# First mixer of a four-stage block: the squares of the queries move from ScalarE to GpSimd, and the first state of the chain of chunks is written with four copies in place of sixteen

## The chip, the core and the metric

The kernel runs on one core of a Trainium2 chip. A core has TensorE (PE; its weight loads are listed as PEld), VectorE (DVE), ScalarE (ACT), GpSimd (POOL) and SyncE (SP), each with an instruction queue of its own, and they meet through semaphores: an instruction can wait for a semaphore to reach a value (`wait_ge`) and can raise one when it ends (`then_inc`). The metric is the time of one execution in microseconds (us). The median of three executions of the kernel before is 836.53 us.

## What is computed

The reference runs four sublayers on 2 sequences of 512 tokens with 256 features, each with a layer norm ahead and a residual sum behind: a mixer with a delta rule, a mixture of experts, a causal attention, and a second mixture of experts. The change lies in the first. There, 16 heads of 16 features:

```python
q = _short_conv(hidden @ Wq, conv_wq)      # conv over 4 tokens, then silu; k and v alike
beta = sigmoid(hidden @ Wb)
q = _l2norm(q) * Dk ** (-0.5)              # x * rsqrt(sum(x*x) + 1e-6) over a head's 16 features
k = _l2norm(k)
def step(S, inp):
    qt, kt, vt, bt = inp
    u = vt - einsum('bhk,bhkv->bhv', kt, S)
    S = S + bt * kt[..., None] * u[..., None, :]
    return S, einsum('bhk,bhkv->bhv', qt, S)
o = _rmsnorm(o, norm_w) * sigmoid(hidden @ Wg)
x = x + o @ Wo
```

The sum of the squares of q that the norm needs is what the moved instructions prepare.

## The kernel before

All instruction streams are written out by hand, one Python function for each engine, and the order in a function is the order in that engine's queue. The first mixer is in `make_attn0`. It cuts the 512 tokens into 32 chunks of 16 and has these stages.

Up to 50 us: projections by TensorE, the short convolution by VectorE, SiLU by ScalarE (`silu_q`, line 2399, writes the queries `qn_`), grams of the chunks. ScalarE, VectorE and TensorE are all full. GpSimd builds masked keys (line 2590) and squares the keys (line 2598), `sq[0]`, with the same operation that the change uses for the queries. Queries and keys stand interleaved in one tile `qk`, so that each is read with a step of two elements.

55 to 92 us, where the change is:
- VectorE runs the elimination, a loop `for m in range(CH + 2)`, which inverts the chunks' triangular systems. Each turn has up to four `tensor_tensor` operations (lines 2780, 2788, 2794 and 2798), all of two inputs from SBUF, with 120 to 512 elements a partition; each waits for a result of the ones ahead of it. The sizes rise to the middle of the loop and fall again.
- TensorE makes the key places, eight groups `u` (line 2227) into banks 6 and 7 in turn, and ScalarE copies each out (line 2454). Among these copies ScalarE has the two squares of the queries, `sq[1]` (line 2457), behind u = 2 and u = 5. Then it takes a square root (line 2459), copies the queries to `qc` (line 2474), which SyncE spreads by 16 DMAs (line 2098), and takes the results of the elimination out of PSUM (`ft_out`, line 2469) and the gates (line 2463).
- TensorE, behind the key places: the first of eight groups of transposes `turn_ft` (line 2251), the sums over the squares (line 2131, 32 matmuls of 8 columns, which wait for `s_sqq`), two further `turn_ft`, and then gates (line 2241) and `turn_ft` in turn. `turn_ft(i)` waits for the turn of the elimination that makes its data; the last waits for VectorE's last step.
- GpSimd clears a tile (line 2612), clears `hdiag` and `seed`, writes `seed`, the first state of the chain (line 2620, 16 copies of 32 partitions x 16 elements, four for each `h`, with a memset of `hdiag` ahead of each four), multiplies for `wz` (line 2626, waits for ScalarE's square root), waits for the gates, and clears `ub` and `place` (lines 2630 and 2631).

From 92 us: `spread(i)` on VectorE, ScalarE and GpSimd (lines 2820, 2501, 2645) waits for the last `ft_out`, for VectorE's small copy at line 2805 and for the sums of the squares, `units(i)` on TensorE (line 2287) waits for the spreads, and then the 32 chunks follow one another in a chain over TensorE, ScalarE and VectorE (lines 2314, 2330, 2863, 2868), to about 190 us. The other three sublayers (`make_rest`) follow.

`ft_out` writes a tile `ftc` that lies over `qk`. So the queries must have been read when the first `ft_out` runs. Before the change all of their readers stand ahead of it in ScalarE's own queue.

Of the kernel before, what the change touches and what calls it, by code (L numbers as in the profile page):

```python
# [11 lines left out]
KD = DIM // P  # L12
# [4 lines left out]
H0, D0, CONV = 16, 16, 4  # L17
# [35 lines left out]
ALU = mybir.AluOpType  # L53
ACT = mybir.ActivationFunctionType
# [1837 lines left out]
def make_attn0(nc, io, sem, sb, arena, bank, rest, g):  # L1892
# [9 lines left out]
    xnT, xn, ident, headmask, w0, wo0, conv_w, norm_w = (  # L1902
        g[n] for n in ("xnT", "xn", "ident", "headmask", "w0", "wo0", "conv_w", "norm_w"))
# [3 lines left out]
    def at(off, n):  # L1907
        assert off + n <= ARENA
        return arena[:, off:off + n]
# [9 lines left out]
    qn_, kc = qk[:, :, :, 0], qk[:, :, :, 1]  # L1919
# [3 lines left out]
    sq = [at(XO + 8192 + NP * t, 2048).rearrange("p (a t) -> p a t", a=KD) for t in range(2)]  # L1923
# [15 lines left out]
    seed = w0f[:, 1024:1280]  # L1939
# [25 lines left out]
    s_siq = sem("a0_siq")  # L1965
    s_siv = sem("a0_siv")
    s_sqk = sem("a0_sqk")
    s_sqq = sem("a0_sqq")
# [118 lines left out]
    class Attn0:  # L2087
# [283 lines left out]
        def act(self, act):  # L2371
# [64 lines left out]
            for i in range(8):  # L2436
# [4 lines left out]
                if g2:  # L2441
# [3 lines left out]
                    for j in range(j0, j0 + 4):  # L2445
                        ins = nc.scalar.copy(ful[1][:, j:CH, :, j].rearrange("p r c -> p c r"), pul[:, j, :, j:CH])
# [5 lines left out]
            for u in range(8):  # L2452
                act.wait_ge(s_kqm, u + 1)
                nc.scalar.copy(kq[:, u, :], bank[6 + u % 2][:]).then_inc(s_kqe, 1)
                if u in (2, 5):
                    act.wait_ge(s_siq, 2)
                    nc.scalar.activation(sq[1][:, u // 3, :], qn_[:, u // 3, :], ACT.Square).then_inc(s_sqq, 1)
            act.wait_ge(s_w, 3)
            nc.scalar.activation(kn[:], rkn[:], ACT.Sqrt).then_inc(s_srk, 1)

# [5 lines left out]
            def ft_out(i):  # L2466
                y, r0, n = i % 2, i // 2 * 4, 2 if i == 7 else 4
                act.wait_ge(s_ft, i + 1)
                nc.scalar.copy(ftc[:, :, y, r0:r0 + n].rearrange("p u r -> p r u"),
                               b_ft[i % 3][:, 0:n * P].rearrange("p (r u) -> p r u", r=n)).then_inc(s_fta, 1)  # L2470

            for a in range(KD):
                for u in range(2):
                    ins = nc.scalar.copy(qc[:, a, :].rearrange("p (n v u x) -> p n v u x", n=NT, v=2, u=2)[:, :, :, u, :],
                                         qn_[:, a, :].rearrange("p (n u v x) -> p n u v x", n=NT, v=2, u=2)[:, :, u, :, :])
            ins.then_inc(s_qc, 1)
            act.wait_ge(s_qc, 1)
            for i in range(3):
                ft_out(i)
            gates(0)  # L2480
# [40 lines left out]
            for c in range(NCH):  # L2521
                t, c8, par, u, s = c // 8, c % 8, c % 2, c // 4, c // 2 % 2
                if c < NCH - 1:
                    for h in range(2):
# [5 lines left out]
                        rows = slice(s * 32, s * 32 + 32)  # L2530
                        src = uo[h][s][rows, 0:256].rearrange("p (j b n) -> p j b n", j=2, b=2)[:, :, 0, :]
                        dst = ub[s][rows, 2 * h:2 * h + 2, 0:64]
                        if par:
                            ins = nc.scalar.activation(dst, src, ACT.Copy, scale=evod[rows, 1:2])
                        else:
                            ins = nc.scalar.copy(dst, src)
# [3 lines left out]
                if par:  # L2540
                    for h in range(2):
# [3 lines left out]
                        for b in range(BATCH):  # L2545
                            o = b * 64 + (1 - s) * 32
                            pr = c8 // 2
                            ins = nc.scalar.copy(
                                fin[t % 2].rearrange("p (b q n) -> p b q n", b=2, q=4)[pr * 32:pr * 32 + 32, b, 2 * h:2 * h + 2, :],
                                uo[h][s][o:o + 32, 0:256].rearrange("p (j b n) -> p j b n", j=2, b=2)[:, :, b, :])  # L2550
# [16 lines left out]
        def act_std(self, act, t):  # L2567
            act.wait_ge(s_fss, 2 * t + 2)
            nc.scalar.activation(fst[1], fst[0], ACT.Sqrt).then_inc(s_fsd, 1)

        def act_turn(self, act, t):
            act.wait_ge(s_ftt, t + 1)
            nc.scalar.copy(fyt, b_fin[:]).then_inc(s_fte, 1)

        def pool(self, pool):
# [8 lines left out]
            for e in range(8):  # L2584
                a, t = e // 4, e % 4
# [3 lines left out]
                for h in KBP:  # L2589
                    ins = nc.gpsimd.tensor_scalar(  # L2590
                        kbd[e % 3][:, :, :, h, :],
                        kc[:, a, :].rearrange("p (b t c j) -> p b t c j", b=BATCH, t=4, c=8)[:, :, t, :, :],
                        hmc(h), 1.0, ALU.mult, ALU.mult)
                ins.then_inc(s_kbp, 1)
                if e in (3, 5):
                    a = (e - 3) // 2
# [7 lines left out]
            for r in range(CH):  # L2604
                ins = pool.memset(ful[0][:, r, :, r:r + 1], 1.0)
# [10 lines left out]
            for h in range(4):  # L2616
                rows = slice(32 * h, 32 * h + 32)
                nc.gpsimd.memset(hdiag[rows, h, :], 1.0)
                for x in range(4):
                    ins = nc.gpsimd.tensor_copy(seed[rows, x * 64 + h * D0:x * 64 + (h + 1) * D0],  # L2620
                                                ident[rows, 32 * h + D0:32 * h + 32])
            ins.then_inc(s_seed, 1)
            pool.wait_ge(s_seed, 1)
            pool.wait_ge(s_rk, 4)
            pool.wait_ge(s_srk, 1)
            nc.gpsimd.tensor_tensor(wz[:], kn[:], beta[:], ALU.mult).then_inc(s_srk, 1)
# [364 lines left out]
```

## Time and profile before

| | |
|---|---|
| median of 3 executions | 836.53 us (835.92 to 839.29) |
| the profiled execution: its time | 836.49 us |
| its span in the trace | 834.7 us |
| busy: TensorE, VectorE, ScalarE, GpSimd | 787.2, 482.1, 360.4, 218.4 us |
| TensorE's granted clock, mean | 0.991 of full |

### The profile page before, as it was taken

Reading aid. Unit: us, or ns where it says so; the run is one execution under the profiler, and the core shown is the slowest. Engines: PE = TensorE matmul, PEld = TensorE weight load, DVE = VectorE, ACT = ScalarE, POOL = GpSimd, SP = SyncE. Lnnn points to the kernel's source line nnn. Section 1 sums busy time; section 2 is a strip of 40 time slices with the busy share of each in tenths; the row PEclk is TensorE's granted clock in tenths of the full one; section 3 lists DMA queues with packets and bytes.
Section 4 is the critical chain, followed back from the end, with each engine's and each line's share of the span. In section 5 each row is a group of like instructions: output and inputs, shape, how many; then the busy total and the mean of one; then the engine's idle time right before and its main releaser. Section 6 shows DMA issues by size and latency. Waiting matters only on the chain.

```text
span 834.7 us, 14393 instructions
## 1 busy us (share of the span) xinstructions
PE 787.2 (94%) x4825; PEld 545.6 (65%) x4825; DVE 482.1 (58%) x1167; ACT 360.4 (43%) x755; POOL 218.4 (26%) x318
## 2 busy tenths in 40 slices
PE   5988799879989998899999999999999999999998
PEld 3576566665657776577777777777764545455557
DVE  5999866766622225865564575967645463324443
ACT  3988777646213324343323343232347666211111
POOL 3644654111610015111211211217712333200000
PEclk9998999999999999999999999999999999999999
DMA  4001790083343312034443232223333433284431
GB/s 145 2 1 29 220 309 1 3 209 101 102 139 103 106 60 82 13 103 135 122 131 93 69 102 69 61 54 99 119 71 114 141 96 110 88 278 126 127 126 50
DMA packets 95807, 85.72 MB, mean 103 GB/s; under 512 B 34792, under 2 KB 84456, under 8 KB 95736
## 3 DMA queue, kind: packets, MB, share of 16 engines
q1 hardware_dynamic: 88200, 70.05, 28.9%
q0 software_dynamic: 4224, 11.74, 4.0%
q10 hardware_dynamic: 3312, 3.02, 1.1%
q8 instruction: 41, 0.67, 0.3%
q14 instruction: 30, 0.25, 0.1%
HBM read 57.02 MB, written 26.71 MB: 100 GB/s over the span
## 4 chain that ended last, share of the span: by engine, by line
PE 79%; DVE 10%; ACT 6%; issue 3%; DMA 1%; SPq 1%; POOL 0%; ACTq 0%; DVEq 0%; POOLq 0%
PE bank L1502 9%; PE bank L1461 8%; PE bank L1320 7%; PE bank L1359 7%; PE bank L1345 6%; PE bank L1281 6%; PE bank L1297 6%; PE bank L744 4%; PE bank L770 3%; PE bank L967 3%; PE bank L2330 3%; PE bank L989 2%; ACT arena L2387 2%; PE bank L2287 2%; PE bank L2314 2%
## 5 line engine op out<-in xcount | busy, mean ns | idle before, releaser
L1619 ACT ACTIVATE arena<-bank 128x512 f32<-128x512 f32 (+1 forms) x96 | 46.8, 525 | 142.7 <-PE bank L1461 142.7
L1243 POOL TENSOR_TENSOR arena<-arena,causal_t 128x256 f32<-128x256 f32 x64 | 45.3, 729 | 208.5 <-ACT arena L1624 207.5
L1502 PEld LDWEIGHTS bank<-arena 128*128 128x128 f32 x640 | 76.2, 191 | 3.9 <-POOL arena L1243 2.3
L1502 PE MATMUL bank<-arena 128*128 128x129 f32 x640 | 77.0, 275 | 1.5 <-POOL arena L1243 1.5
L1461 PE MATMUL bank<-arena 128*128 128x512 f32 (+3 forms) x256 | 74.5, 434 | 1.4 <-DVE arena L1697 1.4
L1554 ACT ACTIVATE arena<-bank 128x512 f32<-128x512 f32 (+1 forms) x39 | 20.2, 520 | 120.7 <-PE bank L1281 111.9
L1320 PE MATMUL bank<-arena 128*128 128x256 f32 (+1 forms) x272 | 66.2, 382 | 3.5 <-DVE arena L1677 3.4
L1281 PE MATMUL bank<-xnT,arena 128*128 128x512 f32 (+1 forms) x168 | 65.9, 514 | 0.0
L1320 PEld LDWEIGHTS bank<-arena 128*128 128x128 f32 (+1 forms) x272 | 50.9, 190 | 21.8 <-issue 10.8
L1359 PEld LDWEIGHTS bank<-arena 128*128 128x128 f32 x256 | 48.3, 190 | 21.6 <-issue 13.6
L1359 PE MATMUL bank<-arena 128*128 128x256 f32 x256 | 60.8, 380 | 1.4 <-issue 0.9
L1345 PE MATMUL bank<-arena 128*128 128x512 f32 x128 | 60.5, 595 | 1.2 <-DVE arena L1695 0.8
L1297 PE MATMUL bank<-xnT,arena 128*128 128x512 f32 (+1 forms) x156 | 61.5, 516 | 0.0
L1461 PEld LDWEIGHTS bank<-arena 128*128 128x128 f32 x256 | 41.3, 191 | 27.0 <-issue 18.5
L1679 DVE TENSOR_TENSOR arena<-arena,bank 128x512 f32<-128x512 f32 (+1 forms) x25 | 15.6, 623 | 68.0 <-PE bank L1297 68.0
L851 POOL DMA_INDIRECT ret<-arena,ridx x32 | 30.7, 960 | 77.0 <-ACT arena L818 60.3
L1693 DVE TENSOR_TENSOR arena<-bank,arena 64x512 f32<-64x512 f32 x36 | 25.0, 693 | 36.7 <-PE bank L1345 26.2
L1297 PEld LDWEIGHTS bank<-xnT,arena 128*128 128x128 f32 x156 | 29.6, 190 | 25.3 <-issue 23.8
L744 PE MATMUL bank<-arena 128*64 (+1 forms) x256 | 44.9, 472 | 0.0
L1704 DVE COPY arena<-bank 128x256 f32<-128x256 f32 x64 | 24.1, 418 | 34.5 <-PE bank L1369 30.8
L2330 PE MATMUL bank<-w,arena 128*128 128x128 f32 x248 | 35.5, 286 | 7.2 <-DVE w L2863 3.3
L1281 PEld LDWEIGHTS bank<-xnT,arena 128*128 128x128 f32 x168 | 31.2, 190 | 16.5 <-issue 14.0
(297 smaller groups left out, 1489.6 us busy)
## 6 DMA issues: line engine op xcount, KB each, us to landing
arena<-in_w_gu SPq DMA_DIRECT2D x44, 256.0 KB, 3.3
rows_in<-place SPq DMA_DIRECT2D x5, 1664.0 KB, 14.6
arena<-in_w_dn SPq DMA_DIRECT2D x34, 128.0 KB, 3.5
rows<-arena SPq DMA_DIRECT2D x8, 544.0 KB, 4.4
arena<-in_w_dn SPq DMA_DIRECT2D x24, 176.0 KB
arena<-in_wq SPq DMA_DIRECT2D x32, 128.0 KB
arena<-in_wo SPq DMA_DIRECT2D x32, 128.0 KB
arena<-rows SPq DMA_DIRECT2D x32, 128.0 KB, 2.0
```

The costliest lines, as they stand in the source:

```text
L744: mm = nc.tensor.matmul(p_gu[J % 2][u * HR:(u + 1) * HR, 0:2 * FE].rearrange("p (y n) -> p y n", y=2), pxT[:, J % 2, k, u * HR:(u + 1) * H ...
L851: nc.gpsimd.indirect_dma_start(ret[h], bass.IndirectOffsetOnAxis(ap=ridx[:, h, j:j + 1], axis=0), py[J % NY], None).then_inc(s_ret, 16)
L1243: nc.gpsimd.tensor_tensor(blocks, blocks, causal_t[:].unsqueeze(1).to_broadcast([P, 2, P]), ALU.mult).then_inc(s_p, 1)
L1281: mm = nc.tensor.matmul(ring(M)[0][:, 0:n], (w_gu, w_gu1)[s][:, slot_of(M), k * P:(k + 1) * P], xnT[:, k, cols], start=(k == 0), stop=(k = ...
L1297: mm = nc.tensor.matmul(ring(M)[1][:, 0:n], (w_gu, w_gu1)[s][:, slot_of(M), (KD + k) * P:(KD + k + 1) * P], xnT[:, k, cols], start=(k == 0 ...
L1320: mm = nc.tensor.matmul(Y[s][half][l // 2][:, (l % 2) * DIM:(l % 2 + 1) * DIM], (hh, hh1)[s][rows, M % 3, j * P:(j + 1) * P], (w_dn, w_dn1 ...
L1345: mm = nc.tensor.matmul(b_q[:], wq[:, n % 2, k, :], xnT2[:, k, b * SEQ:(b + 1) * SEQ], start=(k == 0), stop=(k == KD - 1))
L1359: mm = nc.tensor.matmul(b_y[t // 2][:, (t % 2) * DIM:(t % 2 + 1) * DIM], oT[:, t * P:(t + 1) * P], wo[:, n % 2, :], start=first and t % 2 ...
L1461: mm = nc.tensor.matmul(b_s[sbank][:, o:o + w], kT[:, grp, kt * P:(kt + 1) * P], qr[:, kt * P:SEQ], start=True, stop=True, skip_group_chec ...
L1502: mm = nc.tensor.matmul(b_o[pair][:, t * (DH + 1):(t + 1) * (DH + 1)], pr[:, o:o + P], v[:, grp, kt, :], start=(kt == 0), stop=(kt == qb))
L1619: nc.scalar.activation(th[:, sbank * 512:sbank * 512 + w], b_s[sbank][:, 0:w], ACT.Tanh, scale=SCALE / SOFTCAP).then_inc(s_th, 1)
L2330: mm = nc.tensor.matmul(sacc[h][:, j * P:(j + 1) * P], kq[:, u, hq * P:(hq + 1) * P], ub[s][:, hq, :], start=False, stop=True, skip_group_ ...
```

## The change

In three places of the first mixer:
- ScalarE: the two squares between the key places' copies (line 2457) go. Behind the copies to `qc` a wait for both squares is added (`s_sqq` at 2), ahead of the first `ft_out`.
- GpSimd: the four copies into `seed` for each `h` become one, with the source repeated four times.
- GpSimd: behind the seed copies two `tensor_tensor` multiplications square the queries, 128 partitions x 1024 elements each, ahead of the product for `wz`.

```diff
--- before.py
+++ after.py
@@ -2452,9 +2452,6 @@
             for u in range(8):
                 act.wait_ge(s_kqm, u + 1)
                 nc.scalar.copy(kq[:, u, :], bank[6 + u % 2][:]).then_inc(s_kqe, 1)
-                if u in (2, 5):
-                    act.wait_ge(s_siq, 2)
-                    nc.scalar.activation(sq[1][:, u // 3, :], qn_[:, u // 3, :], ACT.Square).then_inc(s_sqq, 1)
             act.wait_ge(s_w, 3)
             nc.scalar.activation(kn[:], rkn[:], ACT.Sqrt).then_inc(s_srk, 1)
 
@@ -2475,6 +2472,7 @@
                                          qn_[:, a, :].rearrange("p (n u v x) -> p n u v x", n=NT, v=2, u=2)[:, :, u, :, :])
             ins.then_inc(s_qc, 1)
             act.wait_ge(s_qc, 1)
+            act.wait_ge(s_sqq, 2)
             for i in range(3):
                 ft_out(i)
             gates(0)
@@ -2616,11 +2614,13 @@
             for h in range(4):
                 rows = slice(32 * h, 32 * h + 32)
                 nc.gpsimd.memset(hdiag[rows, h, :], 1.0)
-                for x in range(4):
-                    ins = nc.gpsimd.tensor_copy(seed[rows, x * 64 + h * D0:x * 64 + (h + 1) * D0],
-                                                ident[rows, 32 * h + D0:32 * h + 32])
+                ins = nc.gpsimd.tensor_copy(seed[rows].rearrange("p (x h d) -> p x h d", x=4, d=D0)[:, :, h, :],
+                                            ident[rows, 32 * h + D0:32 * h + 32].unsqueeze(1).to_broadcast([32, 4, D0]))
             ins.then_inc(s_seed, 1)
             pool.wait_ge(s_seed, 1)
+            pool.wait_ge(s_siq, 2)
+            for a in range(KD):
+                nc.gpsimd.tensor_tensor(sq[1][:, a, :], qn_[:, a, :], qn_[:, a, :], ALU.mult).then_inc(s_sqq, 1)
             pool.wait_ge(s_rk, 4)
             pool.wait_ge(s_srk, 1)
             nc.gpsimd.tensor_tensor(wz[:], kn[:], beta[:], ALU.mult).then_inc(s_srk, 1)
```

## Rows read from the trace of the kernel before

**Rows 1.** The page, part 4, the chain that ended last, by engine.
```profile
PE 79%; DVE 10%; ACT 6%; issue 3%; DMA 1%; SPq 1%; POOL 0%; ACTq 0%; DVEq 0%; POOLq 0%
```
**Rows 2.** Chain of waits, 57 to 100 us: start us, length us, what.
```profile
89.74 0.29 DVE arena L2798
...
90.08 0.67 PE bank L2251 x4
...
90.77 0.60 DVE arena L2805
...
91.92 1.34 DVE arena L2820 x3
...
93.58 1.07 PE bank L2287 x16
...
94.80 1.07 PE bank L2287 x16
```
**Rows 3.** Timeline: start us, us, engine, line, operation, shapes, [idle before, releaser].
```profile
65.66 2.86 PE L2227 MATMUL bank<-place,arena 128*64 128x256 f32 x24 [1.14 <-ACT arena L2454]
...
71.69 1.08 ACT L2454 COPY arena<-bank 128x512 f32<-128x512 f32 x2
...
72.83 0.65 PE L2251 MATMUL bank<-ident,arena 128*128 128x128 f32 x4 [0.97 <-ACT arena L2454]
...
91.92 0.35 DVE L2820 TENSOR_SCALAR arena<-arena,headmask 128x256 f32<-128x256 f32 x1 [0.56 <-ACT arena L2469]
```
**Rows 4.** Single lines: count, ns min/median/max, first and last start us, forms.
```profile
L2457 ACT ACTIVATE arena<-arena x2: 1187/1194/1200, 67.3 to 70.6; 128x1024 f32<-128x1024 f32 x2
...
L2620 POOL COPY w<-ident x16: 186/516/659, 63.7 to 70.6; 32x16 f32<-32x16 f32 x16
```
**Rows 5.** Timeline, TensorE, sums of squares and transposes.
```profile
73.32 4.70 PE L2131 MATMUL bank<-headmask,arena 128*128 128x8 f32 x32
...
77.88 1.95 PE L2251 MATMUL bank<-ident,arena 128*128 128x128 f32 x8
...
88.82 1.04 PE L2251 MATMUL bank<-ident,arena 128*128 128x128 f32 x8
```
**Rows 6.** Stretches: length, busy PE, PEld, DVE, ACT, POOL, PEclk, DMA share, GB/s.
```profile
75.70:82.50 6.80, 6.80 (x27) 6.26 (x27) 6.70 (x13) 5.24 (x6) 0.00 (x0) 0.50 0.45 71
...
89.40:92.80 3.40, 1.98 (x13) 1.32 (x11) 2.71 (x8) 3.37 (x7) 1.77 (x4) 1.00 0.24 65
```
**Rows 7.** Chain of waits, the start of five turns of the elimination.
```profile
69.95 0.68 DVE w L2780
...
72.33 0.68 DVE w L2780
...
74.78 0.92 DVE w L2780
...
77.50 0.61 DVE w L2780
...
79.88 0.55 DVE w L2780
```
**Rows 8.** GpSimd's groups by form, to 200 us: busy us, mean ns, idle before.
```profile
L2655 POOL TENSOR_TENSOR arena<-arena 128x512 f32<-128x512 f32 x4 | 4.2, 1040 | 22.4 <-ACT arena L2548 22.4
L2598 POOL TENSOR_TENSOR arena<-arena 128x1024 f32<-128x1024 f32 x2 | 3.8, 1890 | 0.0
```
**Rows 9.** Timeline, GpSimd's product and the same VectorE form beside and without it.
```profile
65.65 0.65 DVE L2780 TENSOR_TENSOR w<-arena 128x480 f32<-128x480 f32 x1
...
74.57 0.61 POOL L2626 TENSOR_TENSOR wz<-kn,beta 128x128 f32<-128x128 f32 x1 [3.35 <-ACT kn L2459]
74.78 0.92 DVE L2780 TENSOR_TENSOR w<-arena 128x480 f32<-128x480 f32 x1
```
**Rows 10.** Timeline, a later GpSimd square and the VectorE spread beside it.
```profile
144.97 1.04 POOL L2655 TENSOR_TENSOR arena<-arena 128x512 f32<-128x512 f32 x1 [2.26 <-ACT arena L2548]
...
145.35 0.80 DVE L2820 TENSOR_SCALAR arena<-arena,headmask 128x256 f32<-128x256 f32 x1
```

## The prediction

> **What bounds the kernel now.** I began with the page [rows 1]: a chain of waits that is 79% TensorE and only 10% VectorE. The change touches none of TensorE's long stages, so the share over the whole span says little. I then read the chain of waits between 57 and 100 us, where the edited lines stand. There it is not TensorE. From about 62 us to 90.03 us it is the 60 VectorE steps of the elimination (lines 2780, 2788, 2794, 2798), one waiting for the other, with nothing else in between [rows 2]. Then come the last transpose (90.08, 0.67 us), VectorE's small copy (90.77, 0.60 us), and at 91.92 the first spread of VectorE, with which the chain of chunks starts [rows 2]. All that follows waits for this point and carries a shift of it to the end.
>
> The timeline then says how near the others are. VectorE stood idle for 0.56 us before its first spread, for ScalarE's copy [rows 3]. ScalarE, and TensorE ahead of it, are thus at the same edge as VectorE, late by half a microsecond.
>
> **What the change takes from ScalarE.** Two squares of 128x1024, 1.19 and 1.20 us, which stand in its queue between the copies of the key places [rows 4]. TensorE fills the two banks which these copies empty, and its first transpose (72.83) comes right behind the last copy, which ends at 71.69+1.08 = 72.77 [rows 3]. TensorE took 2.86 us for three of these groups, 0.95 us each, and ScalarE 1.08 us for two copies [rows 3]. Without the squares TensorE's pace of 0.95 us sets the order. Its sixth group, which waited for the first square, then starts at 65.66 + 2.86 = 68.5, and the three groups from there end at 68.5 + 2.86 = 71.4; the last copy ends near 72.0. That is 0.8 us of the 2.39 us, the rest was cover. From there TensorE has work queued without a gap (6.80 us busy of the 6.80 us from 75.7 [rows 6]) to 88.82 + 1.04 = 89.86 [rows 5], so its transposes five and six, and ScalarE's copies of them, come 0.8 us sooner. The seventh needs VectorE's last step and doesn't move. Worth: the 0.56 us that VectorE stood idle, not more, because VectorE's own copy ends at 91.37 whatever ScalarE does [rows 2, 3]. The square root for kn, the gates and the DMA issues behind them also come 0.8 us sooner and nobody on the path waits for them.
>
> **The seed copies.** Sixteen copies took GpSimd from 63.7 to 71.2 us; the shortest 0.19, the middle one 0.52, the longest 0.66 us [rows 4]. So small a copy is mostly waiting for something. Did it cost VectorE anything? The elimination has the same sizes once rising, once falling. The step with 512 and 440 elements went from 69.95 to 72.33, beside copies: 2.38 us. Its mirror, without copies, went from 77.50 to 79.88: 2.38 us [rows 7]. So the twelve that go give VectorE nothing, between 0 and 0.02 us each by the rounding of these rows, and I take 0. On GpSimd they give back 12 x 0.48 = 5.7 us. The four left are four times as long in elements, between 0.19 and 0.66 us each as the old; I take 0.5 us, so that they end near 66 us.
>
> **The two squares on GpSimd.** They start near 66 us, since the queries' SiLU stands in ScalarE's queue far ahead of this stage. The price of one is in the trace: the squares of the keys are the same operation on the same strided form, 1.89 us each [rows 8]. Two end near 70 us, 2 us ahead of TensorE's first transpose and so of the sums that wait for them; the new wait of ScalarE stands behind its copies into the query tile, which come after 72 us, and has been met by then. Queued behind it are all copies of ft_out and the gates. What is queued behind the squares on GpSimd is the product for wz, which waits until 74.57 in any case [rows 9]. By the waits alone the change would gain its 0.56 us.
>
> But VectorE is all this time in operations with two inputs from SBUF. What does GpSimd's reading do to such a one? The trace has one case in this loop. At 74.57 GpSimd multiplied for wz, 128 elements, recorded as 0.61 us and ending at 75.18; the VectorE step recorded at 74.78 took 0.92 us, though the same form took 0.65 us at 65.65 [rows 9]. The pitch shows the same 0.27 us: 74.78 to 77.50 is 2.72 us, its mirror, 72.33 to 74.78, 2.45 us [rows 7]. A second case, later: GpSimd squared 512 elements from 144.97 to 146.01, and VectorE's spread recorded at 145.35 took 0.80 us in place of 0.35 and ended at 146.15, just behind it [rows 3, 10]. A VectorE operation that meets a GpSimd operation starts when that is over. The short copies, too, waited for VectorE's end and not for a turn of their own.
>
> So each square holds VectorE for its length. From 512 elements at 1.04 us and 1024 at 1.89 us [rows 8], one element is 1.66 ns; 896 elements more than the wz product are 1.49 us, and 0.27 + 1.49 = 1.76 us. The longest that it can be is 1.89 us, its whole record. The lower end is 0.27 us, if only the small case's delay recurs. I take 1.76 us, since the second case's delay scales with the operation too. Two squares: 3.52 us on VectorE's chain (0.5 to 3.8).
>
> The Trainium skill says the same in SBUF — State Buffer, section "SBUF: two separate sides": a GpSimd operation and a VectorE operation with two SBUF inputs lock the port pair they share, one of them for its whole instruction, while the other blocks. The two cases above agree; were the port shared by bandwidth instead, the sum would be that of the second rival below.
>
> **The sum.** VectorE's last step ends at 90.03 + 3.52 = 93.55. Transpose, small copy: 90.08 to 91.37 before, so 94.89 now. ScalarE's copy no longer comes last: its fifth and sixth have room now, and the seventh, of half the size, starts with VectorE's small copy and ends with it. First spread: 94.89 in place of 91.92, +2.97 us. The profiled execution took 836.49 us, 1.79 over its span and 0.04 under the median of the runs, 836.53. 836.5 + 3.0 = 839.5. With the end of 3.8: 839.8; with 0.5: 836.4.
>
> **The clock, a term that I can't fix.** Between 75.7 and 82.5 us TensorE had 0.50 of its clock, the lower level of 1.2 GHz, after it had done four transposes and then sums of 8 columns [rows 3, 5, 6]; between 89.4 and 92.8, 1.98 us busy, it kept 1.00, which is 2.4 GHz [rows 6]. In the changed kernel TensorE has little from 88 to 95 us: twelve transposes in 7 us, since it must wait for VectorE. The clock may fall. Eight transposes took 1.95 us at the lower level and 1.04 at the upper [rows 5], so the last four would add 0.5 us on the path: 840.0. I put this in the forecast's range, and take half of it: **839.7 us**.
>
> In the Trainium skill, TensorE: Matmul & The Clock Gate, "What's actually happening", the slow clock is the default and activity releases it. This trace agrees with its 0.50 behind the sums.
>
> **The rivals.**
> *The clock stays low into the first units.* Each of the first units is 1.07 us of TensorE, the second 1.22 us behind the first [rows 2]. At the lower level the first would take 2.1 us, the second starts 0.9 us late, and the spread of the fourth, which waits for the second, by as much to 2 us. With 0.5 us for the transpose: 3.0 + 0.5 + 0.9 to 2.0, 841.4 us (840.9 to 842.5), a slowdown over 0.5% from 1.2 us of it on. For it: the thin stretch is longer than the one that led to 0.50 before. Against it: the chip doesn't drop in every thin stretch, and units come every 1.4 us, so there is slack to catch up.
> *Not slower: VectorE isn't held.* If GpSimd takes elements in turns with VectorE, the squares cost what the sixteen copies did, nothing, and only the 0.56 us is left: 836.0 us (835.5 to 837). It decides if a square costs VectorE under 0.28 us. For it: sixteen copies without any delay. Against it: both cases with more than a hundred elements.
> *GpSimd is held, not VectorE.* Copies of 16 elements ended one per VectorE step; if a square is let in only in pieces, it is stretched, past 74 us, and TensorE's sums wait. Two squares until 76 us would move TensorE by 4 us; transposes five to seven would end near 94 us: 839 to 841 us, hardly to be told from the forecast by time. The product for wz, which got in whole, speaks against.
>
> **How the numbers follow.** Forecast 0.52, clock into the units 0.22, VectorE not held 0.16, GpSimd stretched 0.05, anything else (scatter as in the 839.29 us of one run before, seeds not as thought) 0.05. The forecast's own range is 838.5 to 840.7. To reach 8 in 10 it takes in most of both rivals: 836.0 to 841.7. About 0.5%, 4.2 us, is what a measurement can tell from no change; that line is at 840.7. Slower: nearly all of the clock rival and a little of the forecast, 0.25. Faster: 0.03. Same: 0.72.
>
> **What would show it.** Right: two GpSimd squares of about 1.9 us between 66 and 71 us, two VectorE steps beside them of 2.2 to 2.5 us where 0.5 to 0.7 stood, every other step as before; the last step ends at 93 to 94 us, the first spread at 94.5 to 95.5; ScalarE waits for TensorE ahead of its last ft_out copies. Wrong: VectorE steps unchanged in length; squares over 3 us; the first transpose later than 73 us; or, with all this right, a time that doesn't carry the shift, because a later wait (the rows from DRAM near 246 us) takes it in. That would need a transfer whose start isn't moved by it.

## The result and the profile after

The changed kernel takes 838.95 us (median of 20 executions, 837.73 to 842.32), the kernel before, in the same set, 835.39 us (20 executions, 834.32 to 840.44). The ratio is 1.0043, with a 95% interval of 1.0031 to 1.0054: 3.6 us slower, 2.6 to 4.5. The profiled execution took 837.82 us, of which 836.0 us are span.

The timeline after, at the squares. Columns as in [rows 3].
```profile
64.01 0.40 POOL L2617 COPY w<-ident 32x64 f32<-32x64 f32 x1
...
65.50 4.18 POOL L2623 TENSOR_TENSOR arena<-arena 128x1024 f32<-128x1024 f32 x2
...
65.58 2.34 DVE L2780 TENSOR_TENSOR w<-arena 128x480 f32<-128x480 f32 x1
...
67.85 2.17 DVE L2788 TENSOR_TENSOR w<-arena 128x312 f32<-128x312 f32 x1
...
71.69 0.65 PE L2251 MATMUL bank<-ident,arena 128*128 128x128 f32 x4 [0.68 <-ACT arena L2454]
...
73.40 0.87 POOL L2626 TENSOR_TENSOR wz<-kn,beta 128x128 f32<-128x128 f32 x1 [3.72 <-ACT kn L2456]
```
The step with 480 elements took 0.65 us before [rows 9] and takes 2.34 us now, from just behind the start of the first square to just behind its end; the next, with 312, took 0.48 and takes 2.17 us. Both grew by 1.69 us. The step beside the product for wz is 0.27 us longer than its form, as before the change, and two steps beside the new copies are longer by 0.04 and 0.06 us; no other is. The squares, singly, are recorded with 1.91 us (from 65.50) and 2.31 us (from 67.37).

The chain of waits after, which answers to [rows 2].
```profile
93.06 0.29 DVE arena L2798
...
93.39 1.13 PE bank L2251 x4
...
94.55 0.67 ACT arena L2466
...
95.26 2.07 PE bank L2297 x4
97.33 4.53 PE bank L2287 x64
...
103.31 0.69 PE bank L2314 x16
```
The first spread starts at 95.30 us. The last step of the elimination ends at 93.34 us in place of 90.02. The last transposes take 1.13 us in place of 0.67, since TensorE's clock has fallen:
```profile
89.00:92.30 3.30, 1.31 (x8) 0.84 (x8) 3.14 (x8) 2.02 (x2) 0.23 (x1) 1.00 0.00 0
...
92.30:99.10 6.80, 4.95 (x28) 2.81 (x32) 6.07 (x15) 4.36 (x10) 3.05 (x6) 0.50 0.48 133
```
(columns as in [rows 6]). The low stretch ends at 99.1 us, with the first of the four first units (97.27 to 99.20, 1.93 us in place of 1.07); the other three have the upper level again. And yet the first chunk starts at 103.31 us, where the kernel before had 100.35:
```profile
100.35 0.69 PE L2314 MATMUL bank<-sh,arena 128*64 128x64 f32 x16 [1.30 <-DVE sh L2845]
```
2.96 us later, or 3.10 us reckoned from the start of the elimination, which was 0.14 us earlier in this execution. That is what the profiles show of the change's cost; the 3.6 us of the medians are half a microsecond more, which their interval covers and no row explains. From 103 to 300 us every matmul of the changed kernel runs 2.9 to 3.1 us behind the same one of the kernel before. After 315 us these two profiled executions come nearer, by 1.2 us near 320 us and to 1.3 us at the end. The medians of 20 don't show that, and the last section takes it up.

### The profile page after: what moved, and what is told of

Read it like the earlier page. It is cut to its first block, busy times and chain, and to the rows that moved or that the text cites. A ratio compares the mean times of both kernels' runs of the same rounds, so it can differ in the third digit from the quotient of the medians.

```text
span 836.0 us, 14382 instructions
## 1 busy us (share of the span) xinstructions
PE 788.5 (94%) x4825; PEld 546.1 (65%) x4825; DVE 485.1 (58%) x1167; ACT 359.2 (43%) x753; POOL 217.1 (26%) x308
## 4 chain that ended last, share of the span: by engine, by line
PE 79%; DVE 10%; ACT 6%; issue 3%; DMA 1%; SPq 1%; POOL 0%; ACTq 0%; DVEq 0%; POOLq 0%
PE bank L1502 9%; PE bank L1461 8%; PE bank L1320 7%; PE bank L1359 6%; PE bank L1345 6%; PE bank L1281 6%; PE bank L1297 6%; PE bank L744 4%; PE bank L967 3%; PE bank L770 3%; PE bank L2330 3%; PE bank L989 2%; ACT arena L2387 2%; PE bank L2287 2%; PE bank L2314 2%
```

## The experiments

The theory, called HOLD below: each GpSimd square stops VectorE's chain for nearly its length, 1.76 us; ScalarE's relief gives back half a microsecond; nothing else costs. The rivals: SEED (the new copies are at fault), ENGINE (GpSimd's work or ScalarE's new wait is at fault, wherever it stands), CLOCK (the time goes with TensorE's low clock behind the elimination). As the medians of the kernel before lie up to 2.3 us apart from set to set (835.4 to 837.7), I read two lengths in each profile as well: the elimination (start of the first step at line 2780 to the end of the last at 2798) and from its start to the first chunk (line 2314). The ratios are too wide to tell half the cost from the whole; these lengths carry the argument.

| kernel | squares | elimination, us | start to first chunk, us | ratio to before, 95% interval |
|---|---|---|---|---|
| before | ScalarE | 33.43 | 43.76 | |
| before again | ScalarE | 33.44 | 43.80 | 0.9999 (0.9976 to 1.0022) |
| copies only | ScalarE | 33.49 | 43.71 | 0.9992 (0.9974 to 1.0011) |
| one each | one on either | 35.16 | 45.64 | 1.0018 (1.0001 to 1.0036) |
| after | GpSimd, in the elimination | 36.89 | 46.86 | 1.0043 (1.0031 to 1.0054) |
| after again | same | 36.88 | 46.85 | 1.0034 (1.0015 to 1.0054) |
| squares only | same, 16 seed copies | 36.79 | 46.40 | 1.0034 (1.0012 to 1.0055) |
| eight pieces | same, cut | 36.58 | 47.00 | 1.0059 (1.0038 to 1.0080) |
| one input | same, not squares | 35.25 | 45.70 | 1.0040 (1.0025 to 1.0055) |
| early squares | GpSimd, before it | 33.45 | 43.90 | 1.0005 (0.9986 to 1.0024) |
| placed squares | same | 33.45 | 43.88 | 1.0000 (0.9974 to 1.0025) |
| placed again | same | 33.44 | 43.41 | 1.0002 (0.9979 to 1.0025) |
| filler, large | as after | 36.89 | 48.50 | 1.0080 (1.0051 to 1.0110) |
| filler, fitted | as after | 36.85 | 46.81 | 1.0059 (1.0035 to 1.0083) |

**Copies only.** Of the change, the seed's four copies alone:
```diff
+                ins = nc.gpsimd.tensor_copy(seed[rows].rearrange("p (x h d) -> p x h d", x=4, d=D0)[:, :, h, :],
+                                            ident[rows, 32 * h + D0:32 * h + 32].unsqueeze(1).to_broadcast([32, 4, D0]))
```

> Only the seed is changed: four copies in place of sixteen; the two squares stay on ScalarE. Theory HOLD (each GpSimd square stops VectorE for its length, nothing else of the change costs time): within 0.3 us of the kernel before, VectorE's last elimination step ends at 90.0 us as before. Rival SEED (the fewer, larger copies themselves hold VectorE or come late for the chain): slower by 1 us or more. The larger copies may cost VectorE up to 0.05 us each.

The elimination is 0.06 us longer, the first chunk 0.05 us earlier, the time the same. SEED falls, as far as it meant the copies' own cost.

**One square each**, half the dose:
```diff
+                if u == 2:
+                    act.wait_ge(s_siq, 2)
+                    nc.scalar.activation(sq[1][:, 0, :], qn_[:, 0, :], ACT.Square).then_inc(s_sqq, 1)
...
+            nc.gpsimd.tensor_tensor(sq[1][:, 1, :], qn_[:, 1, :], qn_[:, 1, :], ALU.mult).then_inc(s_sqq, 1)
```

> Half the dose: the first square stays on ScalarE behind the third key-place copy, the second is done by GpSimd; the rest is as in the changed kernel, and TensorE waits for both squares ahead of the sums. Theory HOLD: one VectorE step of about 2.3 us, the elimination ends 1.8 us later than before, half of ScalarE's relief remains; in sum 1.2 to 1.6 us over the kernel before. Rival CLOCK (the time goes with TensorE's low clock behind the elimination, which comes once TensorE waits for VectorE): nearly the whole 3.6 us as soon as the clock falls, or nothing if it stays.

One long step, and the elimination is 1.73 us longer, where two squares made it 3.46 us: the cost goes by the square.
```profile
66.24 2.34 DVE L2783 TENSOR_TENSOR w<-arena 128x480 f32<-128x480 f32 x1
68.51 0.47 DVE L2791 TENSOR_TENSOR w<-arena 128x312 f32<-128x312 f32 x1
```
The ratio, 1.0018, is 1.5 us (0.1 to 3.0). TensorE's clock was low here behind the elimination, from 93.1 to 99.9 us, as in the changed kernel, and the first chunk comes 1.88 us later than in the kernel before, where two squares made it 3.10. CLOCK expected all or nothing.

**Early squares**, the same GpSimd operations 15 to 20 us sooner:
```diff
+            pool.wait_ge(s_siq, 2)
+            nc.gpsimd.tensor_tensor(sq[1][:, 0, :], qn_[:, 0, :], qn_[:, 0, :], ALU.mult).then_inc(s_sqq, 1)
             pool.wait_ge(s_gr, 12)
             pool.memset(ful[0], 0.0).then_inc(s_pz, 1)
+            nc.gpsimd.tensor_tensor(sq[1][:, 1, :], qn_[:, 1, :], qn_[:, 1, :], ALU.mult).then_inc(s_sqq, 1)
```

> Both squares on GpSimd, but 15 to 20 us earlier, one behind the masked keys and one behind the first clearing, where VectorE's operations read PSUM and at most one SBUF input; the wait of ScalarE, the seed copies and the rest as in the changed kernel. Theory HOLD: squares of 1.9 us, no VectorE step lengthened, elimination ends near 90.0 us, 0.5 us faster than the kernel before (835.4 to 834.9). Rival ENGINE (GpSimd's work or the added wait of ScalarE is at fault, wherever it stands): slower than before by 1 us or more.

The elimination has its old 33.45 us, with the squares on GpSimd, ScalarE's wait in place and the four copies. ENGINE falls by these lengths; the time alone, with its interval up to 1.0024, would leave room for it. But the gain of half a microsecond didn't come either; the ratio is 1.0005. VectorE's small scaling at line 2747 took 1.21 us beside GpSimd's clearing of `ful[1]`. I took the second square to have pushed the clearing there, and set out to avoid it next.

**Placed squares**, the second one behind the sixteen small clearings:
```diff
             ins.then_inc(s_pz, 1)
+            nc.gpsimd.tensor_tensor(sq[1][:, 1, :], qn_[:, 1, :], qn_[:, 1, :], ALU.mult).then_inc(s_sqq, 1)
 
             pool.wait_ge(s_const.sem, n_const)
```

> As the early squares, but the second square behind the sixteen small clearings, at 53 us, so that neither clearing moves by more than 1.5 us and none falls on VectorE's small scaling at line 2747. In the early squares the second clearing did, and that scaling took 1.21 us in place of 0.38. Theory HOLD: squares of 1.9 us beside VectorE operations with a PSUM input, none of them longer; line 2747 at 0.3 to 0.4 us; elimination ends at 90.0 us, 0.3 to 0.6 us under the kernel before. Rival ENGINE: slower than before by 1 us or more, with longer VectorE operations beside the squares.

> The same kernel as the placed squares. There, VectorE stood still for 1.37 us in the third pair of chunks, 3.55 us in place of 2.64, with nothing that it waited for; so it did in the early squares and with squares only, not in the other kernels. If that belongs to the kernel (its code's place in memory) it comes back here at the same instruction; if it is chance it doesn't, and the first chunks come 0.4 us sooner than in the kernel before, reckoned from the start of the elimination.

The squares take 1.89 to 1.91 us, nothing beside them is longer (VectorE's copies out of PSUM at line 2710 take 0.59 to 0.64 us, 0.59 to 0.65 in the kernel before), and the elimination has its old length. Yet line 2747 is slow again. Timeline of the second run of it:
```profile
52.69 1.24 DVE L2747 TENSOR_SCALAR wz<-wn 128x128 f32<-128x128 f32 x1
...
52.04 1.80 POOL L2602 MEMSET arena<- 128x2048 f32 x1 [2.47 <-PE bank L2148]
```
The scaling ends at 53.93, just behind the clearing (53.85). The clearing waited 2.47 us for TensorE's grams, so no square had pushed it; TensorE's clock was low at 49.5 to 52.9 us, and the grams were late. My expectation, 0.3 to 0.4 us at that line, missed, and for a reason other than the squares. The early squares had the same reason: there the clearing stood 0.61 us idle behind the second square, for the grams. And one square each and eight pieces, without any early square, show the long scaling as well (1.23 us in both).

In the second run the first chunk comes 43.41 us behind the elimination's start, 0.35 and 0.39 us sooner than in the two runs of the kernel before; in the first run it is 43.88. ScalarE's relief can't be read from this. The first spread comes no sooner than in the kernel before (35.41 us behind the elimination's start in both runs, against 35.33 and 35.32). What differs from the kernel before run again, which also had the low clock there, are the four first units, by the chains of waits of the second run of placed squares and of that run:
```profile
95.17 4.70 PE bank L2287 x64
```
```profile
95.18 5.17 PE bank L2287 x64
```
The low stretch ended 39.6 us behind the elimination's start in the one and 40.4 us in the other, so that the second unit took 1.28 us in place of 1.75. The first run has 4.90 us there and 0.27 us more in VectorE's small copies at line 2845. Neither time differs from the kernel before (1.0000, 1.0002), a gain of 0.3 us can't be told by it, and no version beats the kernel before.

The expectation for the second run asks about a halt of 1.37 us that the first showed in the third pair of chunks, which took 3.55 us in place of 2.63. Chain of waits of the first run:
```profile
108.79 1.37 issue
```
I had read this as VectorE waiting for nothing. The timeline of the same run says otherwise:
```profile
108.56 1.57 DVE L2820 TENSOR_SCALAR arena<-arena,headmask 128x256 f32<-128x256 f32 x1
...
108.78 1.20 POOL L2672 TENSOR_TENSOR arena<-arena,wz 128x256 f32<-128x256 f32 x2
```
VectorE's spread takes 1.57 us, and the two GpSimd products that begin 0.22 us behind its start last 1.20. The second run of the kernel before has the same (and 3.55 us for the pair):
```profile
107.98 1.57 DVE L2820 TENSOR_SCALAR arena<-arena,headmask 128x256 f32<-128x256 f32 x1
...
108.21 1.19 POOL L2672 TENSOR_TENSOR arena<-arena,wz 128x256 f32<-128x256 f32 x2
```
In its first run the products began 0.70 us ahead of the spread, which met only the second of them and took 0.65 us:
```profile
106.02 1.20 POOL L2672 TENSOR_TENSOR arena<-arena,wz 128x256 f32<-128x256 f32 x2
...
106.72 0.65 DVE L2820 TENSOR_SCALAR arena<-arena,headmask 128x256 f32<-128x256 f32 x1
```
In the changed kernel (both runs) and in the second run of placed squares the products begin 0.70 us or more behind the spread's start, and it takes 0.39 to 0.40 us. So this is a hold of the same kind, though the spread reads one tensor and not two, in a place that the change doesn't touch, decided by a few tenths of a microsecond in which of two engines comes first. It is worth 0.9 us in one profile and nothing in the next of the same kernel. No run was made for it alone; it is read from starts and lengths, which agree in all 14 profiles: 1.56 or 1.57 us in the five where the products begin 0.21 to 0.23 us behind the spread, 1.12 us where they begin 0.23 us ahead (one input), 0.65 or 0.66 us in the five where they begin 0.69 or 0.70 us ahead. In all eleven the spread ends 0.14 to 0.16 us behind the products.

**The changed kernel again** and **the kernel before again**, for second profiles:

> The changed kernel itself, beside the others on one chip. Theory HOLD: 3.0 us over the kernel before (2.5 to 3.6), two VectorE steps of 2.1 to 2.4 us, elimination ends 3.3 us later than before. What is open is the scatter: executions of one kernel differ by up to 6 us, and the low stretches of TensorE's clock near 250 and 330 us stand elsewhere in each profile. If these make the scatter, a slow execution has them where TensorE is busy.

> The kernel before, for a second profile of it. Elimination 33.4 us, 10.3 us from its end to the first chunk, 2.62 us for every second chunk at the start of the chain. Open: where the low stretches of TensorE's clock near 230, 250, 330 and 650 us stand in this execution; the theory that they make the scatter expects 1 to 3 us of shift at each one that meets matmuls, and none elsewhere.

Both lengths come back within 0.04 us. For CLOCK the second profile of the kernel before is the plainest test. Its clock was low from 91.4 to 98.3 us, behind the end of the elimination as in the changed kernel, where the first profile of the kernel before had the upper level. The last transposes took 1.06 us in place of 0.67, and the first chunk comes 43.80 us behind the start in place of 43.76. So the low stretch doesn't need the change and moves the first chunk by hundredths. The median on its chip is 840.61 us against 837.71 of the kernel before, which has 35 executions there.

**Squares only**, with the sixteen seed copies left:

> The squares moved as in the change, the seed still written with sixteen copies. GpSimd then reaches the squares at 71 us. Theory HOLD: the two steps held are later ones, each again 2.1 to 2.5 us, the elimination ends 3.3 to 3.6 us later than before, TensorE's sums wait for the squares to 75 us and the time is within 1 us of the changed kernel's. Rival SEED (the copies' saving carries part of the result): slower than the changed kernel by 2 us or more.

GpSimd reaches the squares at 71 us, other steps are held, by the same amount:
```profile
71.57 2.31 DVE L2799 TENSOR_TENSOR arena<-arena,w 128x440 f32<-128x440 f32 x1
73.80 2.37 DVE L2781 TENSOR_TENSOR w<-arena 128x504 f32<-128x504 f32 x1
```
1.70 and 1.69 us more than the 0.61 and 0.68 us of these forms. The squares are recorded with 2.33 and 2.26 us here; the delay of a step is the same. TensorE's sums waited for the squares, by 1.2 us, and that cost nothing, for VectorE is later anyway. The copies give nothing in time, in either direction; they are only what lets the squares come early.

**Eight pieces**, each square cut in four:
```diff
+                for c in range(4):
+                    ins = nc.gpsimd.tensor_tensor(sq[1][:, a, c * 256:c * 256 + 256], qn_[:, a, c * 256:c * 256 + 256],
+                                                  qn_[:, a, c * 256:c * 256 + 256], ALU.mult)
```

> The changed kernel with each square cut in four of 256 elements. Theory HOLD-BY-LENGTH: VectorE's steps and GpSimd's pieces come in turns, each piece holds VectorE for 0.4 to 0.5 us, eight of them 3.3 to 4.0 us; the elimination lasts 36.8 to 37.5 us, no better than whole squares, and VectorE steps of 0.9 to 1.1 us in place of two of 2.2. Rival GAPS (pieces fit beside VectorE's steps as the small seed copies did): elimination under 35 us.

```profile
66.93 1.06 DVE L2783 TENSOR_TENSOR w<-arena 128x480 f32<-128x480 f32 x1
67.92 0.89 DVE L2791 TENSOR_TENSOR w<-arena 128x312 f32<-128x312 f32 x1
```
Steps and pieces in turns, six of the eight steps 0.40 to 0.42 us longer and two 0.29: together 3.15 us of elimination, 0.3 us under the whole squares and just below the range that I had given. Cutting doesn't hide the work. The start of the first chunk, and the ratio, are no better.

**One input.** GpSimd writes max(q, 0) in place of the square, so that this kernel leaves out the squares and its result is not the reference's:
```diff
+                nc.gpsimd.tensor_scalar(sq[1][:, a, :], qn_[:, a, :], 0.0, 1.0, ALU.max, ALU.mult).then_inc(s_sqq, 1)
```

> The changed kernel, but GpSimd writes max(q, 0) into the tile of the squares, an operation with one input in place of the square with two; the squares are left out, so the scaling of the mixer's queries is not the reference's. Theory HOLD-BY-LENGTH (VectorE's two-input step stands still for as long as any GpSimd operation reads SBUF): GpSimd's 256-element operations of this kind took 0.48 us in the kernel before, so 1024 take 0.9 to 1.8 us, and the elimination grows from 33.4 us by twice that less 0.1 to 0.2 us each. Rival TWO-INPUTS (only a GpSimd operation with two inputs holds VectorE): the elimination stays at 33.5 us.

The operation with one input holds VectorE too, so the rival falls:
```profile
65.81 1.58 DVE L2780 TENSOR_TENSOR w<-arena 128x480 f32<-128x480 f32 x1
...
69.97 1.52 DVE L2794 TENSOR_TENSOR arena<-arena,w 128x504 f32<-128x504 f32 x1
```
But not for its length. The steps are 0.93 and 0.84 us longer, the elimination 1.81 us, while GpSimd's records are twice what I expected at most:
```profile
L2623 POOL TENSOR_SCALAR arena<-arena x2: 3752/3916/4079, 65.7 to 69.5; 128x1024 f32<-128x1024 f32 x2
```
Of each 3.8 us VectorE lost 0.9. So "for its length" is right for the square (1.69 us of a record of 1.91) and wrong as a general rule. Whether the rest of this long record is GpSimd waiting for VectorE, or its own work, no run here tells. The time, 1.0040 in five executions, is as long as with whole squares, though the first chunk is only 1.94 us late; the intervals are too wide to set the time against that length.

**Filler.** The changed kernel with matmuls that nobody reads in TensorE's idle time, to keep its clock. The first was too large (19 matmuls; a matmul of this form takes 0.43 us, I had counted half):
```diff
+            for i, n in ((5, 5), (6, 2), (7, 9)):
+                filler(n)
+                turn_ft(i)
+            filler(3)
```

> The changed kernel with 19 matmuls of 256 columns, whose results nobody reads, put into TensorE's idle time ahead of the last three groups of transposes and ahead of the seed products, so that its clock need not fall. Theory HOLD with the clock as an extra: the granted clock stays at 1.00 from 89 to 99 us, the first units take 1.07 us, and what the low clock costs comes back: 0.5 to 1 us under the changed kernel's 838.95, and fewer executions above 840 us. Theory HOLD without clock cost: same as the changed kernel within 0.3 us. Rival CLOCK: back to about 835.4.

The clock stayed at 1.00 and the filler itself held up the last transposes, to 96.78 us. Its time, 1.0080, says nothing on the clock for that reason. The second has 3, 0 and 4 matmuls ahead of the three groups and 1 behind.

> The changed kernel with eight matmuls of 256 columns that nobody reads in TensorE's idle time ahead of the sixth and eighth group of transposes and behind the last, sized to fit (0.43 us each; in the larger filler they held up the transposes by 2 to 3 us). Theory HOLD with clock cost 0.5 us: the granted clock stays at 1.00 from 89 to 99 us, the last transposes take 0.66 in place of 1.11 us, the first spread comes 0.4 us sooner, the chain of chunks 0 to 0.5 us sooner. Rival CLOCK: the chain of chunks starts 2 us or more sooner.

```profile
93.00:99.00 6.00, 4.36 (x42) 2.36 (x42) 5.83 (x14) 4.94 (x12) 4.19 (x9) 1.00 0.60 190
```
The clock is at 1.00, the last transposes take 0.67 us, the first spread comes at 94.74 us in place of 95.30. And the first chunk comes at 103.19 us, 0.12 us sooner than with the low clock. CLOCK falls as far as the first chunk, and so does the half microsecond that I had given to the clock. These rows also show ScalarE's relief: with the upper level as in the kernel before, the first spread comes 1.51 us behind the end of the elimination, where it was 1.90, and the first chunk 9.96 us, where it was 10.33. That is 0.4 us; squares only, at the upper level to 95.6 us, has the same 1.51 us. By its median, though, this kernel is 2.5 us slower than the changed one on the same chip (843.10 and 840.61, 12 executions each). In its profile the loss comes behind 320 us, far from the filler: 1.8 us at the upper level to 330 us and 3.3 us over a low stretch at 331.0 to 337.9 us. Whether the filler brings that about, or one profile is chance, stays open.

## Why the prediction was right

The time was forecast at 839.7 us and came at 838.95; against the kernel before of the same set the change cost 3.6 us where the forecast had 3.2. The low clock term, 0.25 us in that, stood for a cost that isn't there at the first chunk. The absolute time owes something to luck: I had set the kernel before at 836.5, the median of three, and that of 20 is 835.39. Step by step:

- *Squares in the elimination.* Said: 1.76 us each, 3.52 us. Measured: 3.46 us, and 1.73 us for one alone; of the held steps 1.69 us each. The scaling up from a product of 128 elements to a square of 1024 held. That a VectorE operation "starts when that is over" doesn't hold to the letter: the held steps end 0.5 us behind the first square, less than the 0.65 us of their form, and the spreads 0.15 us behind the products, less than their 0.35 us. And of the two cases behind the forecast only the product for wz had a VectorE step with two tensors; the spread reads one. The 1.76 us are shown by the dose of zero, one and two squares, by their move ahead of the elimination, and by their move within it.
- *GpSimd's queue.* Said: copies done near 66 us, squares from 66 to 70. Measured: 65.4, and 65.5 to 69.7. The four copies were shorter than I took them to be, 0.23 to 0.40 us.
- *Seed copies without effect.* Said 0, measured 0.06 us of elimination in copies only, with nothing in the time.
- *ScalarE's relief.* Said: TensorE's first transpose 0.8 us sooner, at most 0.56 us worth. Measured: 71.69 in place of 72.83, 1.14 us sooner, of which 0.16 us are the start of this execution. The key places' six groups took 5.50 us for 48 records, 0.92 us each and not 0.95. Said: at most 0.56 us at the first spread. Measured: 0.39 us, in the two profiles with the upper level there (filler, fitted, and squares only), and nothing at the lower level, in placed squares.
- *First spread.* Said 94.89 in the sum, with 0.5 us more if the clock fell; measured 95.30. The low clock made the last transposes 1.13 us long in place of 0.67. ScalarE's last copy and VectorE's small copy ran beside each other from 94.55 to 95.21 us, as said. At the upper level, in the fitted filler, the spread comes at 94.74.
- *First chunk.* Said +2.97 us by way of the first spread, measured +2.96 us. Here two errors met. At the first spread the shift is 3.38 us. It falls to 2.96 because the four first units, which had gaps before (93.58 to 99.09, 5.51 us), now run back to back in 4.53 us, the first at the lower level and the rest at the upper. I had no term for that.
- *The rival "clock low into the first units"* had the right picture at its start: the clock was low through the first of the four units, the first was late by 3.69 us and the second by 4.17, and nothing of it was left at the first chunk. It had 0.22 of the chance and named 841.4 us; the upper end of its range, 842.5, is 842.0 by its own terms.
- *The rival "GpSimd is held, not VectorE"* falls with the squares of 1.91 and 2.31 us, done at 69.7, and the first transpose at 71.69.
- *The rival "VectorE isn't held"* drew its support from the sixteen small copies. They did tell little of larger operations: no step beside a copy of 16 elements is longer than its form, two beside the copies of 64 are, by 0.04 and 0.06 us.

## What to carry to other kernels

An engine that has time to spare is not free to use. Where the engine on the path reads two SBUF operands, look in the trace for one GpSimd operation beside it, take the delay that it caused, and scale it by the elements of the same kind of operation: here 0.27 us beside 128 elements gave 1.69 us for 1024, while the operation with one input gave 0.9. The same GpSimd work beside VectorE operations that read PSUM lengthened none of them; so place it by what VectorE does at that moment, and not by where GpSimd is idle.

## What the runs showed of the hardware

**A GpSimd clearing holds a VectorE scaling, though not a two-input step.** In all 14 profiles VectorE's `tensor_scalar` at line 2747, from SBUF to SBUF, starts beside the clearing of 2048 elements and ends 0.07 or 0.08 us behind it. It takes 0.37 to 0.39 us in the nine where it starts 0.3 us ahead of the clearing's end, and 1.21 to 1.28 us in the five where it starts earlier in it, so even the short length is no free one. In those five TensorE's clock was low from 50.5 us or earlier and the clearing came late. The elimination's steps beside the clearing of 4096 elements kept their lengths (0.48 us for 312 elements, with it and without). For the two-input steps, held by squares and not by a clearing, the Trainium skill's SBUF — State Buffer, section "SBUF: two separate sides", fits: it limits the lock of a two-input operation to GpSimd operations that read. For the scaling and the spread, which read one tensor, it names another condition, a two-port mode, and no row here shows which mode they run in. Its "whole instruction" doesn't fit the GpSimd operation with one input, which held VectorE for 0.9 of 3.8 us.

**Two GpSimd products in a row hold one VectorE operation through both.** The spread at line 2820 took 1.57 us beside the two, 0.35 us alone, and ended 0.15 us behind the second. And the chain of waits shows such a hold as "issue" with no releaser: only the timeline of both engines names it.

**Where part of the scatter comes from.** Executions of the kernel before lie between 834.2 and 843.0 us, 6 to 8 us apart within one set. Every profile has a few stretches in which TensorE's granted clock is 0.50, and some of them stand elsewhere in each. Two stretches of the copies-only kernel (columns as in [rows 6]):
```profile
246.00:252.40 6.40, 6.07 (x16) 4.20 (x17) 0.67 (x2) 1.44 (x4) 0.00 (x0) 0.50 0.21 63
327.50:331.00 3.50, 3.25 (x9) 2.45 (x10) 1.43 (x5) 0.88 (x3) 2.59 (x4) 0.51 0.33 102
```
and the same place in the kernel before:
```profile
246.30:249.70 3.40, 3.28 (x9) 2.11 (x10) 0.00 (x0) 0.58 (x2) 0.00 (x0) 0.50 0.38 116
249.70:253.00 3.30, 3.30 (x17) 2.57 (x17) 1.14 (x4) 1.07 (x4) 0.00 (x0) 0.99 0.21 62
```
Taking the start of the same matmul in both, the copies-only kernel is 0.34 us ahead at 100 us and 0.09 us ahead at 246 us, then 1.29 us behind at 300 us and 2.80 us behind at 328 us. It loses 1.4 us over the longer low stretch and 1.5 us over the one that the other hasn't. The difference of 2.4 us at the end comes in these two places, of which neither is near the edit.

Other differences come at the upper level. The changed kernel gains 1.2 us on the kernel before near 320 us, where neither has a low stretch. In the changed kernel run again, beside its first profile, 1.6 us are lost ahead of 231.8 us at the upper level and 1.7 us more over a low stretch at 232.2 to 235.7 us; a wait for a transfer at 246 us then takes in 2.9 us of its shift against the kernel before. What makes the losses at the upper level stays open. So a shift met early can be lost or kept later on, and two profiles taken by themselves can show 1.3 us where the medians differ by 3.6.

In a kernel like this the local lengths decide what an edit does, and the medians of many executions decide what it is worth. But each length has its own scatter: the elimination came back within 0.01 us in all three kernels that were profiled twice, and the length to the first chunk within 0.04 us in two of them and only within 0.47 us in placed squares.
